# A three-layer decoder block on one core: turned inputs earlier and in two buffers, spread weight loads, and low parts made by VectorE alone

## The reference

```python
x = _layernorm(x + attn(x, Wqkv, bqkv, Wo, bo))          # A: 16 heads of 16, rotary, causal
x = _layernorm(x + xattn(x, mask, ctx, Wq, Wk, Wv, Wo, gate))   # B: 32 heads of 8, plus tanh(gate)-weighted attention to ctx
x = _layernorm(x + ffn(x, ...))                          # C and D
# ffn: h = x + attn(_layernorm(x));  16 heads of 128, rotary, causal
#      out = h + moe(_layernorm(h)); 4 experts of width 256, the best two, exact gelu
```

## Time and profile before

| | us |
|---|---|
| median of 3 runs | 1220.34 (1218.6 to 1220.37) |
| the profiled execution's own time | 1221.75 |
| its span, first to last instruction | 1220.0 |
| PE busy | 1141.5 (94%) |
| DVE busy | 980.4 (80%) |
| POOL busy | 664.1 (54%) |
| ACT busy | 657.9 (54%) |
| mean granted TensorE clock | 0.987 of full speed |

### The profile page before, as it was taken

The page is one execution under the profiler, slowest core; times in us unless marked ns, Lnnn a source line. Parts: engine busy times, 40 slices in busy tenths (PEclk is TensorE's granted clock), DMA queues, the critical chain, the costliest instruction groups (busy, mean ns, idle before and its releaser), DMA issues.

```text
span 1220.0 us, 29543 instructions
## 1 busy us (share of the span) xinstructions
PE 1141.5 (94%) x11172; PEld 936.5 (77%) x11172; DVE 980.4 (80%) x2274; ACT 657.9 (54%) x1687; POOL 664.1 (54%) x714
## 2 busy tenths in 40 slices
PE   5889999899999999878999999999999999999998
PEld 5666666566676666545799889998999899998886
DVE  5667787879889889877888788887888788868867
ACT  4455564476766766565455444444444444557653
POOL 4656565545545455253677655544554454747665
PEclk9999999999999999999999999999999999999999
DMA  6865543333343333311222000000000100101111
GB/s 165 192 183 125 124 114 86 95 89 106 90 108 98 92 106 91 107 34 41 83 70 71 1 1 2 1 1 2 1 1 1 36 1 1 36 3 36 35 35 35
DMA packets 98558, 76.22 MB, mean 62 GB/s; under 512 B 73547, under 2 KB 86987, under 8 KB 98417
## 3 DMA queue, kind: packets, MB, share of 16 engines
q1 hardware_dynamic: 98417, 74.34, 22.6%
HBM read 53.40 MB, written 19.92 MB: 60 GB/s over the span
## 4 chain that ended last, share of the span: by engine, by line
PE 62%; DVE 21%; issue 7%; ACT 4%; POOL 3%; DMA 1%; SPq 1%; DVEq 0%; POOLq 0%; ACTq 0%
PE bank L1501 5%; PE bank L1502 5%; PE bank L1503 5%; PE bank L1557 4%; DVE B_nr L733 4%; PE bank L1530 4%; PE bank L608 4%; DVE PT L742 3%; PE bank L544 3%; PE bank L471 2%; PE bank L551 2%; PE bank L1572 2%; PE bank L1571 2%; PE bank L1570 2%; PE bank L586 2%
## 5 line engine op out<-in xcount | busy, mean ns | idle before, releaser
L1800 POOL TENSOR_TENSOR C_QK<-C_t1b,C_t2b 128x512 f32<-128x512 f32 x128 | 167.3, 1307 | 229.1 <-DVE C_t2b L1644 228.8
L1641 DVE SCALAR_TENSOR_TENSOR C_t1b<-bank,C_bcol,C_tabs 64x512 f32<-64x512 f32 x256 | 192.0, 750 | 45.9 <-PE bank L1503 41.8
L733 DVE TENSOR_REDUCE B_nr<-bank 128x4 f32<-128x512 f32 x256 | 164.4, 684 | 34.4 <-PE bank L551 33.4
L1501 PE MATMUL bank<-C_XTh,C_Wh 128*128 128x512 f32 x256 | 112.7, 440 | 8.8 <-POOL C_XTl L1490 4.1
L972 ACT ACTIVATE PT<-bank 128x512 f32<-128x512 f32 x160 | 91.9, 597 | 50.1 <-PE bank L586 49.8
L1752 ACT ACTIVATE C_V<-bank 128x512 f32<-128x512 f32 x64 | 38.1, 597 | 132.8 <-PE bank L1519 131.1
L965 ACT ACTIVATE PT<-PT 128x512 f32<-128x512 f32 x96 | 59.4, 630 | 92.5 <-DVE PT L742 92.5
L1733 ACT ACTIVATE C_P<-bank,C_nm 128x128 f32<-128x128 f32 x256 | 90.5, 366 | 25.6 <-DVE C_nm L1654 23.9
L608 PE MATMUL bank<-PT,vpool 128*32 128x128 f32 x2048 | 97.8, 286 | 6.3 <-ACT PT L965 4.4
L1502 PE MATMUL bank<-C_XTl,C_Wh 128*128 128x512 f32 x256 | 101.6, 397 | 0.0
L1503 PE MATMUL bank<-C_XTh,C_Wl 128*128 128x512 f32 x256 | 101.0, 395 | 0.0
(11 more groups left out here) (266 smaller groups left out, 3669.0 us busy)
## 6 DMA issues: line engine op xcount, KB each, us to landing
Adrq<-PB SPq DMA_DIRECT2D x16, 192.0 KB, 2.9
Adrk<-PB SPq DMA_DIRECT2D x16, 192.0 KB, 3.1
stk<-Adrq SPq DMA_DIRECT2D x16, 192.0 KB
stk<-Adrk SPq DMA_DIRECT2D x16, 192.0 KB
Bdrq<-PB SPq DMA_DIRECT2D x16, 192.0 KB, 2.9
stk<-Bdrq SPq DMA_DIRECT2D x32, 96.0 KB
Bdrk<-PB SPq DMA_DIRECT2D x16, 192.0 KB, 2.8
stk<-Bdrk SPq DMA_DIRECT2D x32, 96.0 KB
```

The lines of the kernel that those rows point to most:

```text
L733: e.tensor_reduce(dst, bank[n % 2][:, :].rearrange("p (a b) -> p a b", a=4), AX.X, ALU.max, negate=True).then_inc(sem("m_dve"), 1)
L1501: e.matmul(o[:, :], CWh[hp][:, cs], XCh[0][:, t, :], start=t == 0, stop=False)
L1641: e.scalar_tensor_tensor(out=v4(t1b[kq][lo:lo + 64, :]), in0=v4(o[hi:hi + 64, :]), scalar=bc[hi:hi + 64, :], in1=tabsC[hi:hi + 64, 2 * kq ...
L1800: e.tensor_tensor(QK[v % 3][:, kq, :], t1b[kq][:, :], t2b[kq][:, :], ALU.add).then_inc(sem("rc_pool"), 1)
```

## The change

Six edits:

1. Layer B's loads are spread: weight piece 0 at step 12 as before, piece 1 at step 20, tables and gate at step 24, ctx at step 28; the pieces are split at steps 20 and 27, the tanh of the gate moves to step 40, and two starts of POOL's initialisation (`INITS`) from steps 28 and 32 to 31 and 35.
2. The turns of x for chunks 1 to 7 stand at `bg0 - 4` (before: -2, for chunk 2: -3). Layer A now uses both buffers of XTh and XTl, chunk by chunk in turn, so `x_high` waits for chunk c-2.
3. The first piece of layer A's weights is split one step earlier, ahead of the first x_high and x_low, on ACT and DVE.
4. On ACT `x_high` stands behind `shift` and `evacuate` in a step.
5. In stage C, DVE makes both halves of C_XTl, at r = 14 ahead of the maxima; POOL makes none (before: one). In that step the second half of the rotary products stands ahead of `out_low`.
6. `sums(b)` adds X2 first, and the later of the two expert tiles after it.

```diff
-    LOAD_B, SPLIT_B = 12, (18, 20)
+    LOAD_B, SPLIT_B = (12, 20, 24, 28), (20, 27)
...
-        xts[bg0(c_) - (3 if c_ == 2 else 2)] = (c_, 0)
+        xts[bg0(c_) - (4 if c_ == 1 else 4 if c_ == 2 else 4)] = (c_, 0)
...
         def x_low(c, n):
+            i = n if c > 7 else 1 - c % 2
...
+            if s == 1 - AHEAD:
+                split_weights(0, 0)
             if s == 2 - AHEAD:
-                split_weights(0, 0)
                 split_weights(0, 1)
...
-            if c > 8 or (c and not n):
-                if c < 8:
-                    q.wait_ge("v_pe", 2 * c)
-                    q.wait_ge("pj_pe", k_proj(c - 1, 1) + 1)
...
+            elif c > 1:
+                last = 7 - n if c == 8 else c - 2
+                q.wait_ge("v_pe", 2 * last + 2)
+                q.wait_ge("pj_pe", k_proj(last, 1) + 1)
...
-            if s - 1 in xts:
-                x_high(*xts[s - 1])
             if s - 1 in turned:
                 shift(turned[s - 1])
             if s in evacs:
                 evacuate(*evacs[s])
+            if s - 1 in xts:
+                x_high(*xts[s - 1])
...
-    INITS = {28: (0, 0), 32: (0, 1), 55: (1, 0), 59: (1, 1), 63: (2, 0), 71: (2, 1), 79: (3, 0), 88: (3, 1)}
+    INITS = {31: (0, 0), 35: (0, 1), 55: (1, 0), 59: (1, 1), 63: (2, 0), 71: (2, 1), 79: (3, 0), 88: (3, 1)}
...
+            if r == 14 and u < NU:
+
+                for t in range(2):
+                    xt_low(e, q, c + 1, t)
             if 2 <= u < NU:
                 maxima_c(e, q, u)
-            if r == 14:
-                xt_low(e, q, c + 1, 1)
...
+            if r == 14 and u + 2 < NU:
+                rope_c(e, q, u + 2, 1)
             if 1 <= u <= NU:
                 out_low(u - 1)
...
-            if u + 2 < NU:
+            if u + 2 < NU and r != 14:
                 rope_c(e, q, u + 2, 1)
...
-            if r == 13:
-                xt_low(e, q, c + 1, 0)
...
-            q.wait_ge("t_act", 2 * b + 2)
-            e.tensor_tensor(t0, t0, tD[b % 2][:, 1, :], ALU.add).then_inc(sem("t_pool"), 1)
-            q.wait_ge("t_pool", 2 * b + 1)
+            q.wait_ge("t_act", 2 * b + 1)
             q.wait_ge("x2_pool", 4 * (NCH - 1) + b + 1)
             e.tensor_tensor(t0, t0, X2[(NCH - 1) % 2][:, b, :], ALU.add).then_inc(sem("t_pool"), 1)
+            q.wait_ge("t_act", 2 * b + 2)
+            q.wait_ge("t_pool", 2 * b + 1)
+            e.tensor_tensor(t0, t0, tD[b % 2][:, 1, :], ALU.add).then_inc(sem("t_pool"), 1)
```

More of the change, by code:

```diff
@@ L493, in project @@
             n = 1 if ti == 2 else 0
+            i = n if L else 1 - c % 2
             if hf == 0:
@@ L500, in project @@
                 cs = slice((256 if ti else 0) + hf * 128, (256 if ti else 0) + hf * 128 + 128)
-                m = mm3(o[:, hf * 256:hf * 256 + 256], Wh[L][:, t, cs], Wl[L][:, t, cs], XTh[n][:, t, :], XTl[n][:, t, :],
+                m = mm3(o[:, hf * 256:hf * 256 + 256], Wh[L][:, t, cs], Wl[L][:, t, cs], XTh[i][:, t, :], XTl[i][:, t, :],
                         t == 0, t == 1)
@@ L519, in values @@
             for t in range(2):
-                m = mm3(o[:, 0:256], XTh[n][:, t, xs], XTl[n][:, t, xs], Wh[L][:, t, 512:768], Wl[L][:, t, 512:768], t == 0, t == 1)
+                m = mm3(o[:, 0:256], XTh[i][:, t, xs], XTl[i][:, t, xs], Wh[L][:, t, 512:768], Wl[L][:, t, 512:768], t == 0, t == 1)
             m.then_inc(sem("v_pe"), 1)
@@ L717, in x_low @@
         def x_low(c, n):
+            i = n if c > 7 else 1 - c % 2
             q.wait_ge("xt_act", v_xt(c, n))
-            e.tensor_tensor(XTl[n][:, :, :].rearrange("p a b -> p (a b)"), home["xt", c, n][:, :],
-                            XTh[n][:, :, :].rearrange("p a b -> p (a b)").bitcast(F32), ALU.subtract).then_inc(sem("xt_dve"), 1)
+            e.tensor_tensor(XTl[i][:, :, :].rearrange("p a b -> p (a b)"), home["xt", c, n][:, :],
+                            XTh[i][:, :, :].rearrange("p a b -> p (a b)").bitcast(F32), ALU.subtract).then_inc(sem("xt_dve"), 1)
         def clamp(c):
@@ L864, in x_high @@
         def x_high(c, n):
+            i = n if c > 7 else 1 - c % 2
             q.wait_ge("xt_pe", v_xt(c, n))
-            if c > 8 or (c and not n):
-                if c < 8:
-                    q.wait_ge("v_pe", 2 * c)
-                    q.wait_ge("pj_pe", k_proj(c - 1, 1) + 1)
[L870 to L875, removed]
+            if c > 8:
+                q.wait_ge("v_pe", k_val(c - 1, n, 1) + 1)
+            elif c > 1:
+                last = 7 - n if c == 8 else c - 2
+                q.wait_ge("v_pe", 2 * last + 2)
+                q.wait_ge("pj_pe", k_proj(last, 1) + 1)
+            e.activation(XTh[i][:, :, :].rearrange("p a b -> p (a b)"), home["xt", c, n][:, :], ACT.Copy).then_inc(sem("xt_act"), 1)
         def evacuate(c, ti):
@@ L1008, in act_ab @@
                 split_weights(1, SPLIT_B.index(s))
-            if s == SPLIT_B[1]:
+            if s == 40:
                 q.wait_ge("ld_g", 16)
@@ L1257, in sp_ab @@
                     load_x(c)
-            if s == LOAD_B:
-                for n in range(2):
-                    load_weights(1, n, f"ld_wB{n}", slice(0, 512))
+            if s in LOAD_B[:2]:
+                n = LOAD_B.index(s)
+                load_weights(1, n, f"ld_wB{n}", slice(0, 512))
+            if s == LOAD_B[2]:
                 load(tabsB[:, :, :], I["Btabs"], tabs_ready[1][0])
                 load(gt[:, :], I["Bgate"], "ld_g")
+            if s == LOAD_B[3]:
                 load_ctx(8)
```

## The result

The changed kernel takes 1215.58 us (median of 8 runs, 1214.0 to 1218.37), the kernel before 1220.36 (8 runs, 1218.6 to 1222.22). The ratio is 0.9956, with a 95% interval from 0.9945 to 0.9966. The profiled execution took 1216.62 us, with a span of 1214.8 (before: 1221.75 and 1220.0). The forecast was 1215.0 and, for the profiled execution, 1216.4.

A forecast was written before the change was run, and what follows sets the result against it. PE was taken as the bound, nearly gapless in stage C, with waits in the first layer. Terms -2.8, -3.4, +1.5 and -0.6 sum to -5.3 us: profiled 1221.75 to 1216.4, median 1215.0; range 1210.5 to 1218.5.

The forecast's parts named there:

- signs of being wrong: Unit 16 later than 60.5, half clock after it, or PE waiting for C_nm or C_P in a chunk's unit 15 or 16.
- below 0.9 for C_XTl: Sign of being right: at stage C's chunk boundaries PE's waits for C_XTl are below 0.9 us.
- Unit 16: First layer: the DMA chain for the stacked keys sets unit 16, which comes 0.45 us later; bounds 0 and +0.7.
- Units 16 to 20: First layer: output-copy wait (1.80) and slow stretch (1.7) go, -3.5 us; the XTl wait at 72.14 goes, -0.8.
- Chunks 6 to 8: First layer: new waits for low parts, +0.5 us; last turn's high part behind an evacuation, +0.5; together -0.6 to +2.6.
- The first layer: Sum over unit 16, units 16 to 20 and chunks 6 to 8: -2.8 us.
- My second rival: First layer gives little: gap before unit 16 over 1.5 us, clock falls, new waits; 1217.3 to 1218 us; chance 0.15.
- I take it that it stays: First layer: the clock stays at 1.00 over a gap of about 1.4 us before unit 16; if not, 1.7 us.
- Boundaries: Stage C, three chunk boundaries: C_XTl ready 0.5 us earlier (0.1 at the first), 0.77 C_t2b waits go; -3.4 us.
- End of stage C: At u = 62 later maxima delay exponentials, Gelu and the output PE takes: net +1.5 us, bounds 0.5 and 2.5.
- Tail: End of program: with X2 added first, only one POOL sum is left behind ACT's last tile; -0.6 us.
- The slower rival: Stage C boundaries: late maxima use up DVE's 2.88 us of slack and PE waits; about 1223 us and more; chance 0.06.

The follow-up runs named there:

- last but one experiment: The changed kernel with the first piece of layer A's weights split behind the first high and low parts again: 1218.15 us, ratio to before 0.9972.
- all edits: The changed kernel plus chunk 2's key parts ahead of its query stacks, maxima before DVE's C_XTl halves, chunks 5 and 6 value products a step later: 1212.87 us, ratio 0.9931.

## Why the prediction was right, and where it wasn't

The total was off by 0.6 us; the terms were off by more, in both directions. In the profiled executions the first layer gave 1.6 us less than forecast and the boundaries 0.7 more. The four forecast terms came to -4.4 instead of -5.3, and -0.8 came from places that no term covers. That the total fits so well is luck, all the more since the first layer varies by more than its error. What carried the prediction is stage C: its mechanism was forecast and is borne out by runs of its own. One of the prediction's own signs of being wrong did appear: the clock after unit 16 was half, through unit 17, where it should have been 1.00. And "below 0.9 for C_XTl" held at two boundaries and not at the first (1.37).

- **Unit 16** was forecast 0.45 later and came 0.51 later, held by SP's chain. That is within what varies from run to run (59.2 to 61.7), so the agreement is no proof; that the first split is what delays it was not borne out (last but one experiment). The forecast of the gap ahead of it, 1.4 us with the clock staying, failed: it was 2.97 us, and the clock fell at a price of 2.0 us (+0.51 to +2.53; I had named 1.7 for that case). The step that failed is "about 0.7, the XTl that no longer stands in DVE's step": the whole wait of 1.99 us went, not 0.7 of it, and the slow stretch at 54 us with it, while a new wait of 1.72 us took part of it back. PE was done with its work at 57.06 instead of 59.45.
- **Units 16 to 20**: -3.5 forecast, -3.8 measured from unit 18 to unit 19; -0.8 for the wait at 72.14, -0.8 measured. The size came out right, but not by the forecast path alone: the slow stretch moved ahead of unit 18, where it cost 2.0 us, and the run with the turns alone has the same -3.8 with the old loads. The row of 1.80 us on which the term rests was 0.66 in another profile of the same first layer. What shows edit 1's worth is the run with the split at step 29, 3 us.
- **Chunks 6 to 8**: +0.5 and +0.5 forecast. The two new waits are 1.32 us each, as is their model at 131.34; from unit 22 to unit 44 PE lost 1.14 us. The mechanism was right: the product three places behind the turn waits.
- **The first layer** gave 1.2 instead of 2.8 us in the profiled execution; there the difference is the clock (2.0 us). My second rival had this mechanism. The failed term is "I take it that it stays", the clock over the gap. Since the gap itself came out at 2.97 instead of 1.4 us, the two rows (1.32 and 1.80 us) between which I had placed it did not apply; and the runs above show that no single length from 1.3 to 2.3 us decides the matter (the last section has the cases).
- **Edit 1 needs edit 2, or a later split**, which I had not seen. I costed the split at step 27 at nothing since it "is seven steps of some 2.6 us behind its load"; without edit 2 it costs 2.31 us and the clock. In the combination this doesn't show.
- **Boundaries**: -3.4 forecast, -4.1 measured (1.0, 1.56, 1.57). Of each of the two later ones 0.52 is the shorter wait for C_XTl and 1.00 the other one, which I had counted by its idle time, 0.77; this is the term that was mis-sized. The first has that 1.00 alone, and not the 0.1 that I had added. That DVE is held by POOL's sum was read from one 1.04 us row, and the run with the maxima first shows it.
- **End of stage C**: +1.5 forecast, +1.4 measured (-0.6 for the wait of 0.48, +2.0 behind it), by the path that I gave (maxima 62, norm steps, maxima 63, exponentials, Gelu). With the maxima first the 2.0 are gone.
- **Tail**: -0.6 forecast, -0.4 measured.
- **Not forecast**: the slow stretch moved from 1174 to 1112 us. It cost and gave back the same, so it left the sum alone. Why it stands where it stands is open: the wait ahead of it (0.86 us at 1105.33, before 0.85 at 1109.49) is the same, and the run with the loads alone, whose stages C and D are those of before, has it at 1114 too.

The slower rival did not occur: DVE's idle time at the boundary took up the late maxima (2.87 us before, 0.74 after, at the second boundary), and no PE wait for them shows there.

## What to carry to other kernels

A gain ahead of a point that a DMA queue holds is only a longer wait at that point, and a longer wait can also cost clock behind it: follow the queue's chain (issue, landing, what stands between) before summing up waits. Compare more than one profile of a stretch with much DMA before you price a wait in it. Where small products share a few PSUM banks in turn, moving one changes which product waits for its reader; move the waiting product, not the turn, and look at every step in which a large instruction meets one that PE waits for. An instruction that can't run beside another engine's is best put behind work that can.

## What the runs showed of the hardware that I had not expected

- DVE's copy with two SBUF operands does not run beside POOL's SBUF sum at all: started 0.1 or 0.8 us after the sum, both halves end 1.16 us behind it (2.35 and 1.65 us of busy time for the same work).
- The length of one wait of PE did not tell whether its granted clock would fall. It stayed at 1.00 over 1.35 us (unit 16 with the key parts early), 1.72 us (changed kernel, 44.86) and even 2.33 and 2.02 us (loads alone with the later split), and fell to 0.50 behind 1.80 and 1.99 us (before), 2.31 and 2.97 us. Of two pairs of waits close together, 1.35 and 1.33 us (all edits) and 1.20 and 1.47 us (maxima first), only the first had a fall.
- A wait of PE that the profile prints as 0.77 us cost 1.00 us from start to start, since the matmul behind it no longer overlaps the one ahead.
- Unit 16 varied between 59.2 and 61.7 us over kernels with nearly the same first 40 us; most of it is when SP came to one pair of DMAs (42.8 to 44.6) and how long they took to land (4.3 to 5.7 us).
